# Projected queries of batches 1 to 3 in the bank of the local state

## The reference, cut to what matters

```
q, k, v = h_in @ wq, h_in @ wk, h_in @ wv            # per head
D[t, s] = Fcum[t] - Fcum[s] + i[s]   for s <= t,  m = max_s D
C = (q k^T / sqrt(16)) * exp(D - m)
h = (C / max(|sum C|, exp(-m))) @ v
h_out = sigmoid(h_in @ w_og) * rmsnorm_heads(h)
x1 = x + h_out @ w_out
```

## Time and profile before

| | us |
|---|---|
| three runs | 697.02, 693.39, 696.37 |
| median of the three | 696.37 |
| the profiled execution, its own time | 692.77 |
| span of the profiled execution | 690.9 |
| TensorE matmul (PE) busy | 666.7 |
| VectorE (DVE) busy | 518.5 |
| ScalarE (ACT) busy | 371.5 |
| GpSimd (POOL) busy | 129.3 |

### The profile page before, as it was taken

The page is one execution under the profiler, slowest core; times in us unless marked ns, Lnnn a source line. Parts: engine busy times, 40 slices in busy tenths (PEclk is TensorE's granted clock), DMA queues, the critical chain, the costliest instruction groups (busy, mean ns, idle before and its releaser), DMA issues.

```text
span 690.9 us, 12153 instructions
## 1 busy us (share of the span) xinstructions
PE 666.7 (97%) x4808; PEld 560.5 (81%) x4808; DVE 518.5 (75%) x919; ACT 371.5 (54%) x775; POOL 129.3 (19%) x125
## 2 busy tenths in 40 slices
PE   7989998999999999999999999999899999999996
PEld 7867886878787888878888788887787889889886
DVE  7837879868856667565765676757679998989996
ACT  5887888747543444434443443446565454464541
POOL 7145445300000020000200002000133303203220
PEclk9999999999999999999999999999999999999999
DMA  5088442000210002000010100240000000000000
GB/s 198 5 264 313 108 146 71 1 1 1 63 29 4 1 1 64 1 31 1 1 64 0 32 1 1 93 183 2 0 1 1 0 17 16 1 31 1 1 31 31
DMA packets 24008, 31.27 MB, mean 45 GB/s; under 512 B 1232, under 2 KB 19952, under 8 KB 23184
## 3 DMA queue, kind: packets, MB, share of 16 engines
q1 hardware_dynamic: 23296, 29.18, 12.9%
q10 hardware_dynamic: 656, 1.31, 0.5%
HBM read 28.18 MB, written 2.31 MB: 44 GB/s over the span
## 4 chain that ended last, share of the span: by engine, by line
PE 62%; DVE 22%; ACT 9%; issue 3%; DMA 2%; POOL 1%; SPq 0%; DVEq 0%; ACTq 0%; POOLq 0%
PE bank L94 20%; PE bank L96 19%; PE bank L95 19%; ACT m_W L710 3%; DVE l_ring_lo L2551 3%; DVE l_ge L2532 2%; DVE l_h L2547 2%; DVE l_o L2555 1%; DVE h_raw L1227 1%; DVE l_h L2504 1%; DMA res<-in_x 1%; DVE h_ring_lo L1232 1%; DMA m_W<-m_scratch 1%; PE bank L519 1%; DVE l_oT_lo L2561 1%
## 5 line engine op out<-in xcount | busy, mean ns | idle before, releaser
L1227 DVE TENSOR_TENSOR h_raw<-h_s,bank 128x512 f32<-128x512 f32 x104 | 71.4, 686 | 107.1 <-ACT h_s L1217 92.7
L1217 ACT ACTIVATE h_s<-bank 128x512 f32<-128x512 f32 x104 | 62.2, 598 | 164.6 <-PE bank L96 164.5
L1232 DVE TENSOR_TENSOR h_ring_lo<-h_raw,h_ring_hi 128x512 fp32r<-128x512 f32 x92 | 68.9, 749 | 0.1
L1221 ACT ACTIVATE h_ring_hi<-h_raw 128x512 fp32r<-128x512 f32 x104 | 64.7, 623 | 2.0 <-DVE h_raw L1227 2.0
L95 PE MATMUL bank<-fused_lo,h_ring_hi 128*128 128x256 f32 x208 | 58.4, 281 | 0.0
L2251 ACT ACTIVATE l_s<-bank 128x512 f32<-128x512 f32 x32 | 19.1, 598 | 62.8 <-PE bank L96 62.6
L94 PE MATMUL bank<-l_xT_hi,l_wgu 128*128 128x512 f32 x128 | 51.2, 400 | 0.3
L94 PE MATMUL bank<-f_yT_hi,mlp_hi 128*128 128x512 f32 x128 | 50.6, 396 | 0.0
L95 PE MATMUL bank<-l_xT_lo,l_wgu 128*128 128x512 f32 x128 | 50.0, 391 | 0.0
L96 PE MATMUL bank<-l_xT_hi,l_lo 128*128 128x512 f32 x128 | 50.0, 390 | 0.0
L96 PE MATMUL bank<-f_yT_hi,fused_lo 128*128 128x512 f32 x128 | 50.0, 390 | 0.0
(11 more groups left out here) (372 smaller groups left out, 1970.5 us busy)
## 6 DMA issues: line engine op xcount, KB each, us to landing
m_W<-m_scratch SPq DMA_DIRECT2D x16, 512.0 KB, 6.9
fused_raw<-in_fused SPq DMA_DIRECT2D x1, 3584.0 KB, 12.6
res<-in_x SPq DMA_DIRECT2D x4, 512.0 KB, 6.1
fused_raw<-in_fused SPq DMA_DIRECT2D x2, 1024.0 KB, 9.1
f_mask<-expert_weights SPq DMA_DIRECT2D x8, 256.0 KB
l_raw<-in_layer SPq DMA_DIRECT2D x1, 2048.0 KB, 8.9
out_x<-res SPq DMA_DIRECT2D x16, 128.0 KB, 1.9
f_xw<-in_turned_x SPq DMA_DIRECT2D x3, 512.0 KB, 5.7
```

What stands on the lines that cost most here:

```text
L1217: self.nc.scalar.activation(self.s[u % 2][r, :], gate[r, :], ACT.Silu).then_inc(self.silu.sem, 1)
L1221: self.nc.scalar.activation(self.unit(i, u)[0], self.product(i, u), ACT.Copy).then_inc(self.hi.sem, 1)
L1227: self.nc.vector.tensor_tensor(out=self.product(i, u), in0=self.s[u % 2][r, :], in1=up[r, :], op=ALU.mult).then_inc(self.hidden.sem, 1)
L1232: self.nc.vector.tensor_tensor(out=lo, in0=self.product(i, u), in1=f32(hi), op=ALU.subtract).then_inc(self.lo.sem, 1)
```

## The change

The queries of batches 1 to 3 go to bank 5, as those of batch 0 do. The waits follow the new owners of the banks. project_q(1) waits until the queries of batch 0 have been read (`q_in`, `qt_in`); project_q(2) and project_q(3) wait for the last carry of the batch two before, in place of an add. local_state(b, 0) waits until the queries of batch b + 1 have been read out of bank 5 (for the last batch it keeps its wait). project_v(1, 1) waits for the output gate of batch 0 in place of the queries, and turn_h(0, 1) and turn_h(1, 1) wait for an add in place of the queries of two batches later. No instruction that computes is added, removed or moved in the order.

```diff
--- before.py
+++ after.py
@@ -326,7 +326,7 @@
     rows_banks = [bank[1][0:B * C, 2 * P:3 * P], bank[1][0:2 * B * C, 3 * P:4 * P]]
     side = lambda b, n: bank[(6, 7)[(b + 1 + n) % 2]]
     k_bank = lambda b: side(b, 0) if b else bank[6]
-    q_bank = lambda b: side(b, 1) if b else bank[5]
+    q_bank = bank[5]
     v_bank = lambda b, n: side(b, n) if b else bank[(7, 0)[n]]
     og_bank = lambda b, n: side(b, 1) if b else bank[6 + n]
     hT_bank = lambda b, f: (bank[7], bank[5], bank[6])[f] if b == B - 1 else side(b + 1, f) if f == 0 or b == B - 2 else side(b + 2, 1)
@@ -408,11 +408,12 @@
 
         def project_q(b):
             if b >= 2:
-                pe.wait_ge(added.sem, added.at(b - 2, 1))
+                pe.wait_ge(state_ready.sem, state_ready.at(b - 2, C - 1))
             elif b:
-                pe.wait_ge(og_in.sem, og_in.at(0, 2))
+                pe.wait_ge(q_in.sem, q_in.at(0, 2))
+                pe.wait_ge(qt_in.sem, qt_in.at(0, 1))
             for k in range(KD):
-                last = product(nc, q_bank(b)[:, :], cut(wp, a, k, Qc), cut(yT[b], a, k), k == 0, k == KD - 1)
+                last = product(nc, q_bank[:, :], cut(wp, a, k, Qc), cut(yT[b], a, k), k == 0, k == KD - 1)
             last.then_inc(q_t.sem, 1)
 
         def turn_k(b):
@@ -427,8 +428,7 @@
             elif n == 0:
                 pe.wait_ge(kv_in.sem, kv_in.at(b, KEYS(b)))
             elif b == 1:
-                pe.wait_ge(q_in.sem, q_in.at(b, 2))
-                pe.wait_ge(qt_in.sem, qt_in.at(b, 1))
+                pe.wait_ge(og_in.sem, og_in.at(0, 2))
             else:
                 pe.wait_ge(hT_lo.sem, hT_lo.at(b - 2, 2 * KD))
             for c in (2 * n, 2 * n + 1):
@@ -496,10 +496,11 @@
             if c == 0:
                 pe.wait_ge(kv_in.sem, kv_in.at(b, 3))
                 pe.wait_ge(ktil_ready.sem, ktil_ready.at(b, 1))
-                if b:
+                if b < B - 1:
+                    pe.wait_ge(q_in.sem, q_in.at(b + 1, 2))
+                    pe.wait_ge(qt_in.sem, qt_in.at(b + 1, 1))
+                else:
                     pe.wait_ge(state_ready.sem, state_ready.at(b - 1, C - 1))
-                else:
-                    pe.wait_ge(qt_in.sem, qt_in.at(0, 1))
             elif c == 1:
                 pe.wait_ge(state_ready.sem, state_ready.at(b, 1))
             else:
@@ -533,8 +534,7 @@
                 elif f == 0:
                     pe.wait_ge(added.sem, added.at(b - 1, 2))
                 elif b < B - 2:
-                    pe.wait_ge(q_in.sem, q_in.at(b + 2, 2))
-                    pe.wait_ge(qt_in.sem, qt_in.at(b + 2, 1))
+                    pe.wait_ge(added.sem, added.at(b, 1))
                 else:
                     pe.wait_ge(og_in.sem, og_in.at(B - 1, 2))
             elif f == 0:
@@ -679,7 +679,7 @@
         def copy_q(b):
             act.wait_ge(q_t.sem, q_t.at(b, 1))
             for n in range(2):
-                nc.scalar.activation(q2[b % 2][:, n, :], q_bank(b)[:, :], ACT.Copy, scale=odd_even[:, n:n + 1]).then_inc(q_in.sem, 1)
+                nc.scalar.activation(q2[b % 2][:, n, :], q_bank[:, :], ACT.Copy, scale=odd_even[:, n:n + 1]).then_inc(q_in.sem, 1)
 
         def copy_keys(b):
             act.wait_ge(kv_t.sem, kv_t.at(b, KEYS(b)))
@@ -968,7 +968,7 @@
             dve.wait_ge(q_in.sem, q_in.at(b, 2))
             if b >= 2:
                 dve.wait_ge(intra.sem, intra.at(b - 2, C))
-            nc.vector.scalar_tensor_tensor(out=qt[b % 2][:, :], in0=q_bank(b)[:, P:S], scalar=float(DQ) ** -0.5, in1=eq[:, b, :],
+            nc.vector.scalar_tensor_tensor(out=qt[b % 2][:, :], in0=q_bank[:, P:S], scalar=float(DQ) ** -0.5, in1=eq[:, b, :],
                                            op0=ALU.mult, op1=ALU.mult).then_inc(qt_in.sem, 1)
 
         def weigh_scores(n):
```

## The result

| | before | after |
|---|---|---|
| median of 22 runs, us | 693.47 | 695.94 |
| lowest and highest, us | 692.36, 698.24 | 694.78, 698.06 |
| span of the profiled execution, us | 690.9 | 693.9 |

The ratio of after to before is 1.0029, with a 95% interval from 1.0018 to 1.0039: the changed kernel is slower by 2.0 us (1.2 to 2.7); the two medians lie 2.5 apart. That is inside the 0.5% that the forecast called no change, and outside of zero. The three runs shown ahead of the forecast lay high: their median was 696.37, that of 22 runs is 693.47. The predicted 696.6 is near the measured 695.94 by luck: its base was 2.9 too high and its change 1.8 too small. Against its own base the forecast was +0.2, and the measured change is +2.0, in the two profiled executions +3.0.

A forecast was written before the change was run, and what follows sets the result against it. PE was taken as the bound, busy 666.7 of 690.9 us. Late start +0.60, project_q(2) freed -0.56 and partly covered local_state delays left +0.2 on the median 696.37, making 696.6 us; range 692.5 to 699.0.

The forecast's parts named there:

- The forecast case: Sum of the three places without a clock fall: +0.2 us, 696.6; chance 0.50.
- Rival 1: PE's clock falls in the new gap ahead of project_q(1): 1.3 us more, +1.5 in all, 698.1; chance 0.28.
- the clock: Step on PE's new gap, 41.2 to 44.5: a clock fall might cost 1.3 us, but was left out of the sum.
- Rival 3: Low clock lasts past 50, between 44.5 and 54, and PE becomes the bound: +4.0 us, 700.4; chance 0.04.
- Part 3: Start of the loop: project_q(1) waits for weigh_q(0), 3.28 us late on PE; +0.60 us survives through ACT.
- Part 2: local_state(b, 0) waits for weigh_q(b + 1): 0.30 us late in iterations 1 and 2, covered by 0.27 and 0.26.
- Part 1: project_q(2) no longer stops for DVE's add at line 1053: 0.56 us saved.
- Rival 4: Another wait hides behind the add's, so project_q(2) is not freed: +0.8 us, 697.2; chance 0.10.
- rival 2: ACT absorbs the late start before 54.33, so the wait at project_q(1) costs nothing: -0.4 us, 696.0; chance 0.08.

The follow-up runs named there:

- e10: Changed kernel with score(1) moved ahead of project_q(1), nothing filled in: 1.0014 times the kernel before.
- e8: The changed kernel run once more, unaltered, beside the gap fillings: 1.0020 times the kernel before.
- e2: Kernel before with only the wait added that holds project_q(1) until the queries of batch 0 are read: 1.0037 times the kernel before.
- e3: Changed kernel with the queries of batch 1 back in their side bank, with their old waits: 1.0001 times the kernel before.
- e4: Kernel before with local_state(b, 0) of batches 0 to 2 waiting until the queries of batch b + 1 are read: 1.0008 times the kernel before.
- e9: Changed kernel with four long products (32 rows by 384 columns, of ones) in the gap ahead of project_q(1): 1.0052 times the kernel before.
- e5: Changed kernel with 12 small identity products in the gap ahead of project_q(1): 1.0043 times the kernel before.
- e1: Changed kernel with 24 small identity products (48 matmuls) in the gap ahead of project_q(1): 1.0063 times the kernel before.
- e6: Kernel before with the added wait ahead of project_q(1) and 12 small identity products ahead of it: 1.0028 times the kernel before.
- e12: Kernel before with the added wait ahead of project_q(1) and four long 32-row products in the gap: 1.0036 times the kernel before.
- e11: Second run of the changed kernel with batch 1's queries back in the side bank: 0.9996 times the kernel before, median 693.35 against 693.79 us.

## Why the prediction was right or wrong

**The outcome** was forecast as no change within 0.5%, and 2.0 us is 0.29%. The forecast case, +0.2, did not happen. Rival 1 did, with the clock's fall in the gap at the place named, at a larger price.

**The step that failed** stands under the clock: "The sum above leaves it out, because the fall shown followed a longer thin stretch, while this is one gap behind dense products". One gap of 3.27 us behind dense products was enough, in e10 one of 2.66, and in e8 the clock fell behind one of 1.75. The chances of 0.50 for the sum without it and 0.28 with it were the wrong way round. The rule that the prediction cited from the Trainium skill, page "TensorE: Matmul & The Clock Gate", section "What's actually happening", that the slow clock is the default and activity releases it, agrees with this trace: the clock fell while PE did nothing and came back at 50.3, behind 5.5 us of work. That PE was busy in the profile when it fell in e2, e3, e4, e8 and e9 is more than this short form of the rule tells.

**The size in rival 1** was 1.3 us, taken from a low clock of a few microseconds. Here it lasted 6.8 us, 5.5 of them behind the start of project_q(1), and cost 2.3. The 698.1 given for this rival counts the +0.2 twice: 696.37 + 1.5 is 697.9. In e10, where it lasted 3.4, the mark is 2.06 late, the later copy_q(1) of that order included. Rival 3 described a low clock past 50 at 4.0 us; the clock came back at 50.3, which is its lower edge, and the loss was 2.3.

**Part 3, the wait through ACT's queue,** was forecast at 0.60 and measured at 0.52 in e5, the one trace with the wait in force and a full clock (in e1 and e6 the filling, not the wait, set the start of project_q(1)). With the 0.24 us by which VectorE was early there it is 0.76. Its neighbouring row, 50.21 against the end of project_v(1, 0), was the right one to go by.

**Part 2, local_state behind weigh_q,** came as forecast: 0.32 us of idle time twice, covered but for 0.1 us each time.

**Part 1, the 0.56 us at project_q(2),** came out in number and not in cause. The changed kernel runs 1.36 us there. But so do e2, e6 and e12, which keep the old wait on the add: e12's last product of project_q(2) is at 69.79, 12.25 behind its 57.54, as 69.89 is 12.27 behind 57.62. With PE 3 us late the add is no longer late (the last section shows why). The freed bank can be worth its 0.5 us only where the start is not delayed, as in e11. Rival 4 is out by e11, and rival 2 by the marks.

**What is open.** e5, e9 and e12 have medians above the times of their profiled executions (e9: 697.79 against 695.96), and e5 and e6, whose fillings held the clock in the gap, never got the 2.3 us back in their medians. Stops of PE without a wait, 0.2 to 2.1 us long, appear at 56 to 64 and 113 to 120 in several traces. The number of added matmuls doesn't order them: 48 gave none, 24 up to three. Late instructions would fit, and no run separates that from another cause. What the clock costs is therefore known from the marks of profiled executions, not from a pair of medians.

## What to carry to other kernels

A wait that is put into time in which an engine idles anyway is not free on PE: moving 1.6 us of work from ahead of an idle stretch to behind it made one stretch of 3.3 us, the granted clock fell to half, and that cost three to four times what the wait did (2.3 against 0.5 to 0.8 us). Where the low clock lies decides: ahead of idle time it cost nothing (e3), behind it some 0.4 us for each us. When a bank is given to a new owner, look for the idle time that the new wait makes, not only for who waits behind it. Give the new bank to those users alone whose wait is hidden: here batches 2 and 3 could move at no loss that shows, and batch 1 carried all of it.

## What the runs showed of the hardware

**A filling that kept PE busy and not its clock.** In e9 PE was busy for 2.77 us of the gap with matmuls on 32 rows and 384 columns, and the clock fell to 0.50 at 43.6. In e5, with 2.94 us of matmuls on 128 rows and 128 columns in the same place, it stayed at 1.00. The two kernels differ in this filling alone. One trace each could be chance, but e12 with the filling of e9 shows the same fall (at 43.5), and e1 with 48 of the identity products kept 1.00. The mean granted clock was 0.997 or more in 6 of 12 executions of e5 and 5 of 12 of e6, and in 1 of 12 of e9 and 3 of 12 of e12, but in none of 6 of e1. Rows, columns, number of matmuls and values all differ between the two fillings, and no run says which of them matters.

**A small VectorE instruction waits for GpSimd.** The stop that the change removes from the earlier trace rows seems to go back to this. In the kernel before, POOL and DVE from 60 to 66:

```profile
63.07 1.09 POOL L849 TENSOR_SCALAR_AFFINE_SELECT m_W<-m_W 128x1024 f32<-128x1024 f32 x1
63.08 1.12 DVE L1002 SCALAR_TENSOR_TENSOR m_den<-m_tot 128x16 f32<-128x16 f32 x1
...
65.22 0.68 DVE L1053 TENSOR_TENSOR xn<-bank,xn 128x512 f32<-128x512 f32 x1
```

The instruction on 16 elements (L1002), whose two inputs both come from SBUF, the large on-chip memory, takes 1.12 us and ends with POOL's mask, and the add that releases PE comes at 65.22. In the changed kernel POOL has finished before:

```profile
62.29 1.10 POOL L849 TENSOR_SCALAR_AFFINE_SELECT m_W<-m_W 128x1024 f32<-128x1024 f32 x1 [0.87 <-DVE m_hh L1033]
...
64.54 1.09 POOL L849 TENSOR_SCALAR_AFFINE_SELECT m_W<-m_W 128x1024 f32<-128x1024 f32 x1
...
66.29 0.18 DVE L1002 SCALAR_TENSOR_TENSOR m_den<-m_tot 128x16 f32<-128x16 f32 x1
```

There the same instruction takes 0.18 us. It took 0.18 us in e2, e6 and e12 too, each with POOL idle, and 1.05 and 1.01 in e11 and e4, whose start isn't late and where POOL was at work. That is 0.94 us of VectorE, more than the stop of 0.56, and it would explain why the stop is gone in e2, e6 and e12 with the old wait. The Trainium skill, page "SBUF — State Buffer", section "Who interferes with whom", says that the two engines share a pair of ports under an exclusive lock, and that a VectorE instruction with two SBUF inputs contends with a GpSimd instruction that reads SBUF; the rows agree with that.
